# Which of a chunk's four score groups feeds its maximum to the exponential as a bias: from the first to the third

## The chip, the cores and the metric

The kernel runs on one core of a Trainium2 chip. The metric is the time of one execution on the device in microseconds.

## What is computed

The reference takes x of shape (16, 1024, 256): 16 sequences of 1024 tokens with 256 features. Each of two layers computes `x = x + s * g`, with s an attention and g a SiLU of a feed-forward network, both on the normalised x. The first layer has gated linear attention and eight experts; the second has the attention that the change touches, and a feed-forward network with a squared ReLU. The second attention, cut to what matters:

```python
# 16 query heads of 16, 2 key heads, a window of 64 keys around each query
q = (x @ Wq + bq).reshape(b, s, 16, 16).transpose(0, 2, 1, 3)
k, v = ...                       # 2 heads, padded by 32 on both sides
k_win, v_win = kp[:, :, idx], vp[:, :, idx]      # idx = s + (0..63)
scores = einsum('bgrsd,bgswd->bgrsw', qg, k_win)
probs = softmax(scores, axis=-1)
out = einsum('bgrsw,bgswd->bgrsd', probs, v_win)
return out.reshape(...) @ Wo + bo
```

A softmax row needs its maximum taken off before the exponential; the sum of the exponentials comes out of the product with the values, which carry a column of ones, and is divided out at the end.

## The kernel before

One sequence after the other goes through the whole program. Each engine has its own instruction list, written out by hand in program order (eight sequences are unrolled in the text, and that text runs twice); an engine waits on counted semaphores (`pe.wait_ge(s["pr_ok"], ...)`), each raised by one engine. TensorE's list is the longest; the other engines feed it.

In the second attention a sequence is 8 chunks of 128 tokens. A chunk's scores lie in four PSUM banks, 1 to 4, one for each group j = 0 to 3 of four heads, 96 keys wide for each head. Per chunk:

- TensorE, `score_masks(c)` (L1683): four bf16 matmuls, one for each bank and each on 32 rows of the array, write the window mask; before each it waits until the bank's old scores have been read. Then `score_quad(c)` (L1694): 64 small fp32 matmuls, 16 for each bank, in the order bank 1, 2, 3, 4, bank 1, ...
- VectorE, `shifted(n)` with n = 4c + j: the maximum of each row and head (L1322), and, for three of the four groups, the difference score minus maximum (L1329) into SBUF (`pr`, called am in the profile).
- ScalarE, `exps(n)`: for these three groups one exponential over 128x384 of `pr` in place (L991). For the remaining group, whose maximum was taken negated, four exponentials over 128x96 straight from the bank, with the maximum as the bias (L997), one for each head.
- TensorE, `probs_turn(c, p)` (L1708): transposes groups 0 and 1 (p = 0) or 2 and 3 (p = 1); ScalarE copies the result out in two pieces, `probs_turned` (L1007). TensorE multiplies with the values, `values(c)` (L1727); ScalarE copies that out, `values_out` (L1015); TensorE turns it back, `values_turn` (L1740); VectorE divides by the sums (L1338, L1342).
- TensorE, `attention_turn` (L1747) and `attention_project` (L1753): the output projection, with a ScalarE copy between them, `attention_turned` (L1022).

The seven turns of the loop are in this order. TensorE in turn c: `score_masks(c+1)`, `score_quad(c+1)`, `attention_turn(c-1)`, `probs_turn(c,1)`, `attention_project(c-1)`, `values(c)`, `probs_turn(c+1,0)`, `values_turn(c)`, and for c < 3 `window_values(c+1)` (L1665: eight transposes for the values of later chunks). ScalarE in turn c: `attention_turned(c-1)`, two `probs_turned`, `exps(4c+4)`, `exps(4c+5)`, `values_out(c)`, `exps(4c+6)`, `probs_turned`, `exps(4c+7)`, `probs_turned`. After the loop the feed-forward network begins with `hidden(0, 0)` (L1793, L1798) into the same banks, its ReLU on ScalarE (L1074), the square on GpSimd, a split on ScalarE and VectorE (L1053, L1397), and `project` (L1810).

Of the kernel before, what the change touches and what calls it, by code (L numbers as in the profile page):

```python
# [16 lines left out]
ALU = mybir.AluOpType  # L17
ACT = mybir.ActivationFunctionType
AX = mybir.AxisListType
# [5 lines left out]
NC = S // P  # L25
# [23 lines left out]
def build_program(nc, a, out, n_seq):  # L49
# [3 lines left out]
    def sb(name, shape, dt=F32):  # L53
        return ctx.enter_context(nc.sbuf_tensor(name, shape, dt))

    def sem(name):
        return ctx.enter_context(nc.semaphore(name))
# [129 lines left out]
    row_max = sb("row_max", [P, 4, 4])  # L187
# [101 lines left out]
    s = {n: sem(n) for n in names}  # L289
# [36 lines left out]
    def at(name, value=0):  # L326

        return now["copy"] * per_sequence[name] + value
# [379 lines left out]
    with nc.Fori(0, n_seq // UNROLL) as turn:  # L708
        with nc.Block() as block:
# [124 lines left out]
            def _(act):  # L834
                for copy in range(UNROLL):
# [150 lines left out]
                    def exps(n):  # L986

                        c, j = n // 4, n % 4
                        if j:
                            act.wait_ge(s["sub_ok"], at("sub_ok", 3 * c + j))  # L990
                            nc.scalar.activation(pr[:, j], pr[:, j], ACT.Exp).then_inc(s["pr_ok"], 1)  # L991
                            return
                        act.wait_ge(s["max_ok"], at("max_ok", n + 1))
                        if c:
                            act.wait_ge(s["ptp_ok"], at("ptp_ok", 4 * c - 2))
                        for h in range(4):
                            ins = nc.scalar.activation(pr[:, j, h, :], bank[1 + j][:, h * KW:(h + 1) * KW], ACT.Exp,  # L997
                                                       bias=row_max[:, j, h:h + 1])
                        ins.then_inc(s["pr_ok"], 1)
# [18 lines left out]
                    def attention_turned(c):  # L1018
                        act.wait_ge(s["o2tp_ok"], at("o2tp_ok", c + 1))
                        if c:  # L1020
                            act.wait_ge(s["s2p_ok"], at("s2p_ok", c))
                        nc.scalar.copy(o2t[:], bank[0][:, 0:D])\  # L1022
                          .then_inc(s["o2t_ok"], 1)

                    exps(0)
                    queries_keys(3)
                    exps(1)
                    queries_keys(4)
                    exps(2)
                    queries_keys(5)  # L1030
                    exps(3)
# [83 lines left out]
            def _(dve):  # L1115
                for copy in range(UNROLL):
# [198 lines left out]
                    def shifted(n):  # L1315

                        c, j = n // 4, n % 4
                        scored = bank[1 + j][:, 0:4 * KW].rearrange("p (h k) -> p h k", k=KW)
                        dve.wait_ge(s["sc_ok"], at("sc_ok", n + 1))
                        if j == 0 and c:  # L1320
                            dve.wait_ge(s["pr_ok"], at("pr_ok", 4 * c - 3))
                        nc.vector.tensor_reduce(row_max[:, j, :], scored, AX.X, ALU.max, negate=(j == 0))\  # L1322
                          .then_inc(s["max_ok"], 1)
                        if j == 0:
                            return
                        dve.wait_ge(s["max_ok"], at("max_ok", n + 1))
                        if c:
                            dve.wait_ge(s["ptp_ok"], at("ptp_ok", 4 * (c - 1) + 2 * (j // 2) + 2))
                        nc.vector.tensor_tensor(pr[:, j], scored, row_max[:, j, :].unsqueeze(2).broadcast_to([P, 4, KW]),  # L1329
                                                ALU.subtract).then_inc(s["sub_ok"], 1)  # L1330
# [15 lines left out]
                    def attention_bias(c):  # L1346
                        dve.wait_ge(s["s2p_ok"], at("s2p_ok", c + 1))
                        nc.vector.tensor_tensor(attn2[:, c, :], bank[0][:, D:2 * D], bc_o2[:], ALU.add)\
                          .then_inc(s["s2_ok"], 1)

                    shifted(0)
                    window_values(0)
                    for n in range(1, 4):
                        shifted(n)
                    for c in range(NC - 1):
                        shifted(4 * c + 4)
                        shifted(4 * c + 5)
                        shifted(4 * c + 6)
                        if c:
                            attention_bias(c - 1)  # L1360
                        shifted(4 * c + 7)
                        attention_out(c)
                        if c < 3:
                            window_values(c + 1)
                        if c in (1, 2):

                            g = c - 1
                            nc.vector.tensor_copy(xh[:, g], xt[:, :, g * 512:(g + 1) * 512]).then_inc(s["xh_ok"], 1)  # L1368
                        if 3 <= c < 7:
                            low_split((c - 3) // 2, (c - 3) % 2)  # L1370
# [55 lines left out]
            def _(pe):  # L1426
                for copy in range(UNROLL):
# [247 lines left out]
                    def score_masks(c):  # L1675

                        for j in range(4):
                            if c and j == 0:
                                pe.wait_ge(s["pr_ok"], at("pr_ok", 4 * c - 3))
                            elif c:  # L1680
                                pe.wait_ge(s["sub_ok"], at("sub_ok", 3 * c - 3 + j))
                            rows = slice(j * WB, (j + 1) * WB)
                            nc.tensor.matmul(bank[1 + j][:, 0:4 * KW], four_bf[rows, :],  # L1683
                                             band_q[rows, :].unsqueeze(1).broadcast_to([WB, 4, KW]),
                                             start=True, stop=False, skip_group_check=True)
# [81 lines left out]
                    chunk_turn(NC - 1)  # L1767
                    pe.wait_ge(s["qk2_ok"], at("qk2_ok", 4))
                    score_masks(0)
                    score_quad(0)  # L1770
                    window_values(0)
# [5 lines left out]
                    def hidden(n, part):  # L1777

                        g, m = n // MT, n % MT
                        h_bank = bank[1 + n % 3][:]  # L1780
                        if part == 0:
                            if n >= 3:
                                pe.wait_ge(s["relu_ok"], at("relu_ok", n - 2))
                            else:
                                if n == 0:
                                    pe.wait_ge(s["pr_ok"], at("pr_ok", 4 * NC - 3))
                                else:
                                    pe.wait_ge(s["sub_ok"], at("sub_ok", 3 * NC - 3 + n))
                            if m == 0:
                                pe.wait_ge(s["xl_ok"], at("xl_ok", g + 1))  # L1790
                            for t in (xh, xl):
                                for k in range(KD):
                                    nc.tensor.matmul(h_bank, fc_t[:, k, m * P:(m + 1) * P], t[:, g, k, :],  # L1793
                                                     start=(t is xh and k == 0), stop=False)
                        else:
                            if m == 0:
                                pe.wait_ge(s["tst_ok"], at("tst_ok", g + 1))
                            nc.tensor.matmul(h_bank, u_t[:, m * P:(m + 1) * P], t_st[:, g, :], start=False, stop=True)\  # L1798
                              .then_inc(s["h2p_ok"], 1)
# [29 lines left out]
                    for c in range(NC - 1):  # L1829
                        score_masks(c + 1)  # L1830
                        score_quad(c + 1)
                        if c:
                            attention_turn(c - 1)
                        probs_turn(c, 1)
                        if c:
                            attention_project(c - 1)
                        else:
                            low_rank(1)
                        values(c)
                        probs_turn(c + 1, 0)  # L1840
                        values_turn(c)
                        if c < 3:
                            window_values(c + 1)
                    hidden(0, 0)
                    hidden(0, 1)
                    attention_turn(NC - 2)
                    probs_turn(NC - 1, 1)
                    hidden(1, 0)
                    hidden(1, 1)
                    attention_project(NC - 2)  # L1850
# [62 lines left out]
```

## Time and profile before

| | |
|---|---|
| time, three runs | 3715.4, 3718.62 and 3726.18 us, median 3718.62 |
| the profiled execution | 3713.08 us, of it 3711.4 us span |
| TensorE matmuls busy | 92% of the span |
| VectorE, ScalarE, GpSimd busy | 68%, 52%, 34% |
| granted TensorE clock | 0.994 on average |

Busy time is the time in which an engine runs instructions; the span is from the first instruction to the last. The granted clock is a share of full speed.

### The profile page before, as it was taken

Reading aid. Unit: us, or ns where it says so; the run is one execution under the profiler, and the core shown is the slowest. Engines: PE = TensorE matmul, PEld = TensorE weight load, DVE = VectorE, ACT = ScalarE, POOL = GpSimd, SP = SyncE. Lnnn points to the kernel's source line nnn. Section 1 sums busy time; section 2 is a strip of 40 time slices with the busy share of each in tenths; the row PEclk is TensorE's granted clock in tenths of the full one; section 3 lists DMA queues with packets and bytes.
Section 4 is the critical chain, followed back from the end, with each engine's and each line's share of the span. In section 5 each row is a group of like instructions: output and inputs, shape, how many; then the busy total and the mean of one; then the engine's idle time right before and its main releaser. Section 6 shows DMA issues by size and latency. Waiting matters only on the chain. (4 is left out here: it accounts for less than half of the span.)

```text
span 3711.4 us, 89270 instructions
## 1 busy us (share of the span) xinstructions
PE 3420.2 (92%) x34684; PEld 2299.6 (62%) x34684; DVE 2515.5 (68%) x6040; ACT 1928.1 (52%) x4295; POOL 1279.9 (34%) x1489
## 2 busy tenths in 40 slices
PE   3999999999999999999989999999999999999998
PEld 2666666666666666666656666666666666666666
DVE  4666776667677666677656776677666767676667
ACT  2365462645636465463644636546364563646546
POOL 3523324232342423325223251332424234242332
PEclk9999999999999999999999999999999999999999
DMA  3101010010100101001010010101001010010100
GB/s 86 24 14 46 2 39 20 14 46 2 47 13 18 42 14 35 13 24 35 14 36 13 24 35 14 47 2 38 21 15 45 2 47 13 18 42 14 35 13 24
DMA packets 91022, 97.16 MB, mean 26 GB/s; under 512 B 19824, under 2 KB 73696, under 8 KB 90592
## 3 DMA queue, kind: packets, MB, share of 16 engines
q1 hardware_dynamic: 90592, 91.35, 9.1%
q8 instruction: 279, 4.57, 0.5%
q14 instruction: 151, 1.24, 0.1%
HBM read 74.01 MB, written 17.30 MB: 25 GB/s over the span
## 5 line engine op out<-in xcount | busy, mean ns | idle before, releaser
L827 POOL TENSOR_TENSOR qx<-qx 128x512 f32<-128x512 f32 x256 | 278.1, 1091 | 680.3 <-ACT qx L1074 679.4
L1322 DVE TENSOR_REDUCE row_max<-bank 128x4 f32<-128x384 f32 x512 | 271.9, 549 | 134.7 <-PE bank L1694 134.2
L1202 DVE TENSOR_TENSOR am<-bank,causal 128x512 f32<-128x512 f32 x512 | 327.2, 680 | 43.2 <-PE bank L1543 43.2
L1397 DVE TENSOR_TENSOR sq_lo<-qx,sq_hi 128x512 fp32r<-128x512 f32 x256 | 208.0, 813 | 198.4 <-ACT sq_hi L1053 197.9
L925 ACT ACTIVATE tanh_g<-bank 128x256 f32<-128x256 f32 x128 | 49.1, 383 | 468.4 <-PE bank L1432 468.4
L1432 PE MATMUL bank<-w_vg,xt 128*128 128x512 f32 x512 | 253.9, 618 | 0.0
L821 POOL TENSOR_TENSOR xl<-xt,xh 128x1024 fp32r<-128x1024 f32 x32 | 75.3, 2354 | 469.2 <-DVE xh L1368 469.2
L1473 PE MATMUL bank<-xt,w_down 128*128 128x512 f32 x512 | 235.5, 592 | 0.0
L1810 PE MATMUL bank<-sq_hi,pj_t 128*128 128x512 f32 x512 | 214.7, 419 | 16.4 <-DVE sq_lo L1397 9.9
L1329 DVE TENSOR_TENSOR am<-bank,row_max 128x384 f32<-128x384 f32 x384 | 214.0, 557 | 13.1
L744 POOL TENSOR_TENSOR qx<-qt,par_mask 128x512 f32<-128x512 f32 x128 | 139.2, 1088 | 194.9 <-ACT qt L447 155.4
L991 ACT ACTIVATE am<-am 128x384 f32<-128x384 f32 x384 | 206.4, 538 | 0.0
L1074 ACT ACTIVATE qx<-bank,scale_fc 128x512 f32<-128x512 f32 x256 | 177.3, 693 | 50.7 <-PE bank L1798 50.7
L1708 PE MATMUL bank<-ident,am 64*96 64x64 f32 x4096 | 166.9, 221 | 38.8 <-ACT am L991 24.1
L1810 PE MATMUL bank<-sq_lo,pj_t 128*128 128x512 f32 x512 | 202.2, 395 | 0.0
L1708 PEld LDWEIGHTS bank<-ident,am 64*96 64x96 f32 x4096 | 130.5, 123 | 104.1 <-issue 54.3
L1053 ACT CAST sq_hi<-qx 128x512 fp32r<-128x512 f32 x256 | 158.9, 621 | 67.4 <-PE bank L1810 36.8
L940 ACT ACTIVATE tanh_f<-bank 128x256 f32<-128x256 f32 x128 | 49.3, 385 | 239.6 <-PE bank L1574 239.6
L1543 PE MATMUL bank<-qx,k 32*128 32x256 f32 x2048 | 146.6, 400 | 28.2 <-ACT k L844 17.8
L1793 PE MATMUL bank<-xh,fc_t 128*128 128x512 f32 x512 | 171.2, 415 | 0.0
L1694 PE MATMUL bank<-k,qt 32*32 32x192 f32 x8192 | 164.1, 332 | 0.0
L1793 PE MATMUL bank<-xl,fc_t 128*128 128x512 f32 x512 | 160.3, 394 | 0.0
(258 smaller groups left out, 8709.1 us busy)
## 6 DMA issues: line engine op xcount, KB each, us to landing
g_wide<-gate_rows SPq DMA_DIRECT2D x64, 512.0 KB, 6.5
qt<-in_L_attn_x SPq DMA_DIRECT2D x136, 128.0 KB, 2.3
x<-in_L_attn_x SPq DMA_DIRECT2D x128, 128.0 KB, 2.2
out<-x SPq DMA_DIRECT2D x128, 128.0 KB, 1.7
x<-in_L_ffn_w_fc SPq DMA_DIRECT2D x1, 1024.0 KB, 5.6
attn<-in_L_ffn_w_proj SPq DMA_DIRECT2D x1, 1024.0 KB, 7.9
w_up<-in_L_ffn_Wu SPq DMA_DIRECT2D x1, 512.0 KB, 5.8
w_down<-in_L_ffn_Wd SPq DMA_DIRECT2D x2, 256.0 KB, 3.5
```

The source lines that it names most:

```text
L827: nc.gpsimd.tensor_tensor(sq[:, n % 3, :], relu[:, n % 3, :], relu[:, n % 3, :], ALU.mult)\
L991: nc.scalar.activation(pr[:, j], pr[:, j], ACT.Exp).then_inc(s["pr_ok"], 1)
L1074: nc.scalar.activation(relu[:, n % 3, :], bank[1 + n % 3][:], ACT.Relu, scale=scale_fc[:, n % MT:n % MT + 1]).then_inc(s["relu_ok"], 1)
L1202: nc.vector.tensor_tensor(am_tiles[:, :, j], bank[3 + j][:].rearrange("p (f e t) -> p f e t", f=2, e=2), causal[:].unsqueeze(1).unsqueeze( ...
L1322: nc.vector.tensor_reduce(row_max[:, j, :], scored, AX.X, ALU.max, negate=(j == 0))\
L1329: nc.vector.tensor_tensor(pr[:, j], scored, row_max[:, j, :].unsqueeze(2).broadcast_to([P, 4, KW]), ALU.subtract).then_inc(s["sub_ok"], 1)
L1397: nc.vector.tensor_tensor(sq_lo[:, n % 3, :], sq[:, n % 3, :], sq_hi[:, n % 3, :].bitcast(F32), ALU.subtract)\
L1432: mm = nc.tensor.matmul(dst, xt[:, k, c * P:(c + 1) * P], w[:, k, :], start=(k == 0), stop=(k == KD - 1))
L1473: mm = nc.tensor.matmul(bank[5 if g else j][:], w_down[:, k, j * P:(j + 1) * P], xt[:, k, g * 512:(g + 1) * 512], start=(k == 0), stop=(k ...
L1708: mm = nc.tensor.transpose(bank[5 + r][0:KW, h * QB:(h + 1) * QB], pr[rows, 2 * p + h // 4, h % 4, :], ident[rows, rows])
L1793: nc.tensor.matmul(h_bank, fc_t[:, k, m * P:(m + 1) * P], t[:, g, k, :], start=(t is xh and k == 0), stop=False)
L1810: mm = nc.tensor.matmul(bank[5 + o][:], pj_t[:, m, o * P:(o + 1) * P], part[:, n % 3, :], start=(m == 0 and part is sq_hi), stop=(m == MT ...
```

## The change

The group that takes its maximum as a bias, and so needs no difference on VectorE, is j = 2 where it was j = 0. For group 0 VectorE now computes the difference, and its exponential is one instruction; for group 2 the difference goes, and its exponential is four instructions from PSUM bank 3. The waits follow: a mask for bank 3 (and, after the last chunk, the first matmul of `hidden(2, 0)`) waits for ScalarE's exponential, the one for bank 1 for VectorE's difference. The order in which the groups come on each engine stays.

```diff
@@ exps(n) on ScalarE
                         c, j = n // 4, n % 4
-                        if j:
-                            act.wait_ge(s["sub_ok"], at("sub_ok", 3 * c + j))
+                        if j != 2:
+                            act.wait_ge(s["sub_ok"], at("sub_ok", 3 * c + min(j + 1, 3)))
                             nc.scalar.activation(pr[:, j], pr[:, j], ACT.Exp).then_inc(s["pr_ok"], 1)
                             return
                         act.wait_ge(s["max_ok"], at("max_ok", n + 1))
                         if c:
-                            act.wait_ge(s["ptp_ok"], at("ptp_ok", 4 * c - 2))
+                            act.wait_ge(s["ptp_ok"], at("ptp_ok", 4 * c))
                         for h in range(4):
                             ins = nc.scalar.activation(pr[:, j, h, :], bank[1 + j][:, h * KW:(h + 1) * KW], ACT.Exp,
                                                        bias=row_max[:, j, h:h + 1])
@@ shifted(n) on VectorE
                         dve.wait_ge(s["sc_ok"], at("sc_ok", n + 1))
-                        if j == 0 and c:
-                            dve.wait_ge(s["pr_ok"], at("pr_ok", 4 * c - 3))
-                        nc.vector.tensor_reduce(row_max[:, j, :], scored, AX.X, ALU.max, negate=(j == 0))\
+                        if j == 2 and c:
+                            dve.wait_ge(s["pr_ok"], at("pr_ok", 4 * c - 1))
+                        nc.vector.tensor_reduce(row_max[:, j, :], scored, AX.X, ALU.max, negate=(j == 2))\
                           .then_inc(s["max_ok"], 1)
-                        if j == 0:
+                        if j == 2:
                             return
@@ score_masks(c) on TensorE
                         for j in range(4):
-                            if c and j == 0:
-                                pe.wait_ge(s["pr_ok"], at("pr_ok", 4 * c - 3))
+                            if c and j == 2:
+                                pe.wait_ge(s["pr_ok"], at("pr_ok", 4 * c - 1))
                             elif c:
-                                pe.wait_ge(s["sub_ok"], at("sub_ok", 3 * c - 3 + j))
+                                pe.wait_ge(s["sub_ok"], at("sub_ok", 3 * c - 3 + min(j + 1, 3)))
@@ hidden(n, 0) on TensorE
-                                if n == 0:
-                                    pe.wait_ge(s["pr_ok"], at("pr_ok", 4 * NC - 3))
+                                if n == 2:
+                                    pe.wait_ge(s["pr_ok"], at("pr_ok", 4 * NC - 1))
                                 else:
-                                    pe.wait_ge(s["sub_ok"], at("sub_ok", 3 * NC - 3 + n))
+                                    pe.wait_ge(s["sub_ok"], at("sub_ok", 3 * NC - 2 + n))
```

On ScalarE, one whole turn of the loop, from the copy of `attention_turned` to the last `probs_turned`. Before:

```order
L1022 COPY o2t<-bank 128x256
L1007 COPY xn<-bank 96x8x64 x2
L997 ACTIVATE am<-bank,row_max 128x96 x4
L991 ACTIVATE am<-am 128x384
L1015 COPY o_turned<-bank 128x4x4x32
L991 ACTIVATE am<-am 128x384
L1007 COPY qx<-bank 96x8x64
L991 ACTIVATE am<-am 128x384
L1007 COPY qx<-bank 96x8x64
```

With the change, the same turn:

```order
L1022 COPY o2t<-bank 128x256
L1007 COPY xn<-bank 96x8x64 x2
L991 ACTIVATE am<-am 128x384 x2
L1015 COPY o_turned<-bank 128x4x4x32
L997 ACTIVATE am<-bank,row_max 128x96 x4
L1007 COPY qx<-bank 96x8x64
L991 ACTIVATE am<-am 128x384
L1007 COPY qx<-bank 96x8x64
```

The four small exponentials have moved from ahead of `values_out` (o_turned) to behind it; what stood behind them up to `values_out` now follows one exponential, and what follows the third group's exponential now follows four.

On VectorE, the four groups of one chunk, from the first maximum up to the division for the chunk before (the row L1348 is the bias of the output projection). Before:

```order
L1322 TENSOR_REDUCE row_max<-bank 128x4 x2
L1329 TENSOR_TENSOR am<-bank,row_max 128x384
L1322 TENSOR_REDUCE row_max<-bank 128x4
L1329 TENSOR_TENSOR am<-bank,row_max 128x384
L1348 TENSOR_TENSOR attn<-bank,bc_o 128x256
L1322 TENSOR_REDUCE row_max<-bank 128x4
L1329 TENSOR_TENSOR am<-bank,row_max 128x384
L1338 RECIPROCAL rden<-bank 128x16
```

With the change:

```order
L1322 TENSOR_REDUCE row_max<-bank 128x4
L1329 TENSOR_TENSOR am<-bank,row_max 128x384
L1322 TENSOR_REDUCE row_max<-bank 128x4
L1329 TENSOR_TENSOR am<-bank,row_max 128x384
L1322 TENSOR_REDUCE row_max<-bank 128x4
L1348 TENSOR_TENSOR attn<-bank,bc_o 128x256
L1322 TENSOR_REDUCE row_max<-bank 128x4
L1329 TENSOR_TENSOR am<-bank,row_max 128x384
L1338 RECIPROCAL rden<-bank 128x16
```

The difference of the first group now stands ahead of the second group's maximum, and the third group's difference is gone; five instructions still stand ahead of L1348. TensorE's instructions and their order are the same.

## Rows read from the trace of the kernel before

**Rows 1.** Page, part 1: busy time of the engines, share of the span, instructions
```profile
PE 3420.2 (92%) x34684; PEld 2299.6 (62%) x34684; DVE 2515.5 (68%) x6040; ACT 1928.1 (52%) x4295; POOL 1279.9 (34%) x1489
```

**Rows 2.** Page, part 4: the chain that ended last, by line
```profile
PE bank L1473 3%; PE bank L1571 3%; PE bank L1432 2%; PE bank L1793 2%; PE bank L1708 2%; PE bank L1654 2%; PE bank L1694 2%; PE bank L1614 2%; PE bank L1453 2%; ACT am L997 2%; DMA g_wide<-gate_rows 1%; PE bank L1810 1%; PE bank L1543 1%; PE bank L1528 1%; PE bank L1740 1%
```

**Rows 3.** Waits: engine, line, whom it waited for; total us, times, longest
```profile
PE bank L1708 <- ACT am L991: 24.1, 96, 0.3
```

**Rows 4.** Timeline, turn c = 5 and the next: start us, length us, engine, line
```profile
246.78 1.02 DVE L1322 TENSOR_REDUCE row_max<-bank 128x4 f32<-128x384 f32 x2
247.83 0.56 DVE L1329 TENSOR_TENSOR am<-bank,row_max 128x384 f32<-128x384 f32 x1
...
248.70 1.03 ACT L997 ACTIVATE am<-bank,row_max 128x96 f32<-128x96 f32 x4
...
248.86 1.08 PE L1727 MATMUL bank<-xn,v 96*32 96x128 f32 x32
...
249.60 0.54 ACT L991 ACTIVATE am<-am 128x384 f32<-128x384 f32 x1
...
250.02 0.59 ACT L1015 COPY o_turned<-bank 128x512 f32<-128x512 f32 x1
...
250.19 0.65 PE L1708 MATMUL bank<-ident,am 64*96 64x64 f32 x16 [0.25 <-ACT am L991]
250.28 0.56 DVE L1329 TENSOR_TENSOR am<-bank,row_max 128x384 f32<-128x384 f32 x1
250.49 0.54 ACT L991 ACTIVATE am<-am 128x384 f32<-128x384 f32 x1
...
250.77 0.66 PE L1740 MATMUL bank<-ident,o_turned 128*128 128x128 f32 x4
...
251.36 0.34 PE L1683 MATMUL bank<-band_q,four_bf 32*128 32x384 bf16 x4
...
251.63 1.28 PE L1694 MATMUL bank<-k,qt 32*32 32x192 f32 x64
...
253.22 0.65 PE L1708 MATMUL bank<-ident,am 64*96 64x64 f32 x16
```

**Rows 5.** Timeline, turn c = 0 of the same sequence
```profile
216.44 1.08 PE L1727 MATMUL bank<-qx,v 96*32 96x128 f32 x32
...
217.45 0.65 PE L1708 MATMUL bank<-ident,am 64*96 64x64 f32 x16
217.59 0.58 ACT L1015 COPY o_turned<-bank 128x512 f32<-128x512 f32 x1
...
218.23 0.65 PE L1740 MATMUL bank<-ident,o_turned 128*128 128x128 f32 x4
```

**Rows 6.** Timeline, turn c = 1, where window_values follows values_turn
```profile
223.05 1.08 PE L1727 MATMUL bank<-xn,v 96*32 96x128 f32 x32
...
224.97 0.66 PE L1740 MATMUL bank<-ident,o_turned 128*128 128x128 f32 x4
...
226.13 0.34 PE L1683 MATMUL bank<-band_q,four_bf 32*128 32x384 bf16 x4
```

**Rows 7.** Timeline, turn c = 6, the last, and what follows it
```profile
255.02 1.08 PE L1727 MATMUL bank<-qx,v 96*32 96x128 f32 x32
...
257.97 0.60 ACT L1007 COPY xn<-bank 96x512 f32<-96x512 f32 x1
...
258.90 0.65 PE L1708 MATMUL bank<-ident,am 64*96 64x64 f32 x16
```

**Rows 8.** Timeline, the one named wait of TensorE in the feed-forward network, 259 to 282 us
```profile
278.02 0.50 PE L1810 MATMUL bank<-sq_hi,pj_t 128*128 128x512 f32 x1 [0.24 <-DVE sq_lo L1397]
```

**Rows 9.** Timeline, the sequence's first chunk: its third exponential, and the next masks
```profile
209.86 0.51 ACT L991 ACTIVATE am<-am 128x384 f32<-128x384 f32 x1
...
211.47 0.34 PE L1683 MATMUL bank<-band_q,four_bf 32*128 32x384 bf16 x4
```

## The prediction

> **What bounds the kernel now.** The page's busy shares come first: TensorE is busy for 92% of the span, the next engine for 68% [rows 1]. So a change is worth what it does to the start times of TensorE's instructions, and nothing else. The chain that ended last runs mostly through TensorE's lines, and one line that the change moves stands in it: L997, the four small exponentials, with 2% of 3711 us, some 74 us [rows 2]. It is one of the few places where ScalarE, not TensorE, sets the pace. The waits then say how much of that is idle time: TensorE waits before the transposes of `probs_turn` (L1708) for the exponential L991 in 96 places, 24.1 us in all, 0.25 us each [rows 3]. 96 is 16 sequences by six of the loop's seven turns. The timeline of one turn says why, and what comes after it; all that follows is read from there.
>
> Take T as the start of `values(c)` on TensorE, 248.86 in turn 5 [rows 4]. ScalarE begins the four small exponentials at 248.70 and ends them at 249.73; the second group's exponential ends at 250.14, and `probs_turn(c+1,0)` starts 0.05 us later, at 250.19. The values' matmuls had ended at 249.94. That is the 0.25 us. But behind `probs_turn` TensorE needs `values_out`, which ScalarE can't begin before the values are done: 250.02 to 250.61. `values_turn` starts at 250.77, only 0.16 us after it. The masks start at 251.36 (T + 2.50), the scores at 251.63, and 6.16 us after T the next values start, at 255.02 [rows 7].
>
> **The change, part by part.**
>
> Work: VectorE still has four maxima and three differences a chunk, ScalarE four small and three large exponentials, TensorE the same list. Nothing is added or removed; only times move.
>
> (a) The first two exponentials. They cost 0.54 us each where the first cost 1.03, with 0.42 us from one start to the next (249.60 to 250.02) [rows 4]. If ScalarE begins at 248.70 as before, the second ends at 248.70 + 0.42 + 0.54 = 249.66, before the values' end at 249.94, so the 0.25 us wait is gone. Condition: VectorE must have both differences ready. The first maximum starts at 246.78; two maxima take 1.02 us, a difference 0.56 [rows 4]. Maximum, difference, maximum, difference at 0.56 us each at most end by 249.02. ScalarE wants the second difference at 249.12. The cover is 0.1 us, and behind it the 0.28 us by which the exponential is now early (249.66 against 249.94); it holds.
>
> (b) What TensorE gets of the 0.25 us. `values_turn` can't start before `values_out` is copied, and turn 0 shows what happens without the wait: `probs_turn` starts with the values' end, at 217.45, ScalarE copies from 217.59, and `values_turn` starts at 218.23, 1.79 us after the values [rows 5]. With the wait it is 1.91 (248.86 to 250.77) or 1.92 (223.05 to 224.97) [rows 4, 6]. So the gain is 0.13 us a turn, half of the wait.
>
> (c) What the third group's exponential now holds. It starts 0.47 us after `values_out`'s start, at T + 1.63 (250.49). Before, no one on TensorE waited for it: the last difference on VectorE, 250.28 to 250.84, had freed the last bank, half a microsecond before the masks. Now it is four instructions, 1.03 us, to T + 2.66, and the mask for bank 3 may start at T + 2.71. Before, the masks started at T + 2.50 [rows 4]. Behind this mask in TensorE's list stand the fourth mask, the 64 score matmuls, and all of the next turn. So where nothing stands between `values_turn` and the masks, they come 0.21 us late, with the gain of (b) already eaten. These are the masks behind turns 3, 4 and 5: three in a sequence. The first two masks go ahead at T + 2.37. That could help only if the scores could then follow in less than the 0.27 us that they now stand behind the masks (251.36 to 251.63). The profile gives the four masks as one group of 0.34 us, so I read them as running side by side, each for most of the 0.34, and the 0.27 us as running time, not issue time. I take the whole 0.27 again behind the late mask. The lower bound: a quarter of it for each of two masks, 0.13, so 0.07 us late instead of 0.21. The upper bound: the two late masks don't run together any more but one behind the other, another 0.27: 0.48 us late.
>
> The Trainium skill, TensorEngine Tiling (Array Packing), Key Properties, says that changing the tiling mode drains the engine, and also that tiles within a mode load and run independently. Masks are 32x128 and scores 32x32, so by the first rule no score starts before the late mask is through: 0.21 us. By the second alone the scores of banks 1 and 2 would run ahead, and the cost would be near the lower bound. The trace agrees with the first as far as it goes, with its 0.27 us between masks and scores [rows 4].
>
> (d) Turns 1 and 2. There `window_values` stands between `values_turn` and the masks, which start at T + 3.08 (223.05 to 226.13) [rows 6]. Moved up by 0.13 they start at T + 2.95, still after T + 2.71. So these turns keep the gain: twice -0.13. If that cover were gone it would cost +0.21 there as well.
>
> (e) Turn 0 has no wait to lose, and keeps its time [rows 5]. The first chunk: its third exponential, 209.86 to 210.37, would last to 210.89, and the masks start at 211.47 [rows 9]; nothing.
>
> (f) Turn 6. Behind it come the first hidden matmuls, which need bank 1, free early. But `probs_turn(7,1)` needs the fourth `probs_turned` copy, to clear its banks. Before, that copy starts at T + 2.95 and ends at T + 3.55 (257.97, 0.60), and the transposes start at T + 3.88 (258.90) [rows 7]. Now the copy stands behind four small exponentials, that is 0.90 - 0.42 = 0.48 us later (248.70 to 249.60 is the step behind four small ones, 249.60 to 250.02 that behind a large one [rows 4]): it ends at T + 4.02, the transposes start at T + 4.07. So +0.19. In turns 3 to 5 the same copy is also late, but there `probs_turn(c+1,1)` stands at T + 4.36 (253.22) [rows 4], which has cover of 0.3 us, and more once the masks are late. The feed-forward network behind it shows TensorE with one named wait up to 282 us, 0.24 us [rows 8]; it is fed by a chain that starts from TensorE too, so I let the delay run through.
>
> Sum for a sequence: -0.13 x 2 + 0.21 x 3 + 0.19 = +0.56 us; by 16, +9.0 us. Against the profiled execution: 3713.1 + 9.0 = 3722.1. That execution lies 5.5 us under the median of the runs shown, 3718.6; against the median it is 3727.6, and I say 3727. It is +0.24%; about 0.3%, 11.2 us, is what a measurement of this kernel can tell from no change.
>
> **Rivals.**
>
> Forecast (54%): the gains of two turns, the losses of three and of the end. Its own range: with 0.17 to 0.27 for the held masks, +7 to +12 us, so about one case in four of it lies above 0.3%.
>
> Held masks are cheap (15%): 0.07 us instead of 0.21. Sum -0.26 + 0.21 + 0.19 = +0.14, by 16 +2 us: 3721. For it speaks that two of the four masks and their rows of the array are free early; against it, that the scores of the late rows need as long as the others' and are issued in order.
>
> Faster (8%): the third exponential holds no one, because it starts earlier than I have it. Then six turns give 0.13 us each, by 16 -12.5 us: 3706; were the whole wait to come off, -24.1 [rows 3], 3694. It decides if that exponential ends 0.2 us earlier than T + 2.66. Against it: `values_out` stands ahead of it and waits for the values' end.
>
> Slower, the masks torn apart (15%): the wait in the middle of the four masks costs more than its length, 0.48 us a time by the upper bound. That is 0.27 x 3 x 16 = +13 us on top, +22 in all: 3740. For it speaks that the four now start as one group; against it, that the third and fourth are still released together. It passes 0.3% from 0.26 us for a held mask (the sum is then -0.26 + 0.78 + 0.19 = +0.71, by 16 +11.4).
>
> Slower, the first wait stays (8%): the second difference on VectorE comes over 0.4 us later than I have it, since the first is now ahead of it, and `probs_turn` waits on. The gain of turns 1 and 2 is gone: (0.63 + 0.19) x 16 = +13 us: 3732.
>
> **How the numbers follow.** Slower by over 0.3%: 0.15 + 0.08 + a quarter of 0.54, 0.36. Faster: 0.08. Within: 0.56. The range from 3711 to 3739 leaves out the faster rival and the last microsecond or so of the torn masks, and holds the cheap masks (3721), the forecast and the wait that stays (3732). It goes 10 us below the cheap masks and 7 above the stayed wait, since the three runs before lie 11 us apart.
>
> **What the profile after would show.** The 96 waits of L1708 for L991 gone; in turns 1 to 6 `values_turn` 1.79 us behind the values. A new wait at the masks L1683 for L997, 48 times, some 0.2 to 0.35 us each (the first masks at T + 2.37, the rest at T + 2.71), and a distance between values of turns 3 to 6 of 6.37 us where it was 6.16, and 0.13 us less in turns 1 and 2. L1708 after turn 6 waiting for a copy of L1007, 16 times, 0.2 to 0.3 us. I am wrong if the masks start within 0.05 us of T + 2.50 in turns 3 to 5, if their wait is there and the scores still follow at T + 2.84 or earlier, or if the feed-forward network gives the delay back before the sequence ends.

## The result: slower, by more than the moved waits

The changed kernel takes 3755.18 us (median of four, 3751.93 to 3757.93), the kernel before 3719.7 (median of four): a ratio of 1.0094, with a 95% interval from 1.0076 to 1.0111. The prediction was 3727, from 3711 to 3739. It had the direction; the measured loss, 35 us, is about four times the forecast one. The profiled execution takes 3757.93 us, 3756.2 of it span, 44.8 us more span than before.

The profile after, first by the same views. The page, part 1, and from part 5 the matmuls of L1571 in the first layer; then the same group before, which was not shown above (busy us, mean ns of one, idle before it):

```profile
PE 3470.1 (92%) x34684; PEld 2330.9 (62%) x34684; DVE 2515.7 (67%) x6040; ACT 1940.4 (52%) x4295; POOL 1279.9 (34%) x1489
...
L1571 PE MATMUL bank<-w_up,qx 128*128 128x256 f32 x512 | 134.5, 410 | 33.5 <-POOL qx L786 33.5
```

```profile
L1571 PE MATMUL bank<-w_up,qx 128*128 128x256 f32 x512 | 125.4, 389 | 32.7 <-POOL qx L786 32.7
```

TensorE has the same 34684 matmuls, but is busy for 50 us more [rows 1]. Idle time is not what grew. And matmuls in another layer, which the change doesn't touch, have become longer, while they wait for GpSimd hardly longer than they did. That is the first sign that something beside the waits has moved.

The waits (engine, line, whom for; total us, times, longest):

```profile
PE bank L1708 <- ACT qx L1007: 14.7, 16, 0.9
PEld bank L1683 <- ACT am L997: 12.2, 48, 0.3
...
PE bank L1708 <- ACT xn L1007: 5.4, 16, 0.3
```

The 96 waits of [rows 3] are gone. The 48 waits before the masks are there, 0.25 us each, and the 16 behind turn 6, 0.34 us each. The first of the three rows is the old wait in turn 0, with the same 14.7 us as before.

The timeline of TensorE in turns 1 to 4 and 6 answers to [rows 4, 6, 7]:

```profile
223.46 1.08 PE L1727 MATMUL bank<-xn,v 96*32 96x128 f32 x32
...
230.07 1.08 PE L1727 MATMUL bank<-qx,v 96*32 96x128 f32 x32
...
236.68 1.08 PE L1727 MATMUL bank<-xn,v 96*32 96x128 f32 x32
...
238.47 0.66 PE L1740 MATMUL bank<-ident,o_turned 128*128 128x128 f32 x4
239.05 0.68 PE L1683 MATMUL bank<-band_q,four_bf 32*128 32x384 bf16 x4
239.67 1.28 PE L1694 MATMUL bank<-k,qt 32*32 32x192 f32 x64
...
243.05 1.08 PE L1727 MATMUL bank<-qx,v 96*32 96x128 f32 x32
...
255.79 1.08 PE L1727 MATMUL bank<-qx,v 96*32 96x128 f32 x32
...
259.96 0.65 PE L1708 MATMUL bank<-ident,am 64*96 64x64 f32 x16 [0.34 <-ACT xn L1007]
```

From T = 236.68 of turn 3: `values_turn` at T + 1.79, the masks from T + 2.37 and now 0.68 us long as a group, since two of them wait in the middle and start at T + 2.72 (the row of their weight load below); the scores at T + 2.99, 0.22 later than T + 2.77 before; the next values at T + 6.37, where it was 6.16. Turn 1 lasts 6.61 us (6.74 before, from 223.05 to 229.79). Behind turn 6 the transposes stand at T + 4.17.

```profile
239.40 0.09 PEld L1683 LDWEIGHTS bank<-band_q,four_bf 32*128 32x128 bf16 x2 [0.26 <-ACT am L997]
```

So the moved waits do almost what the prediction says. They explain a quarter of the loss. The rest shows when the granted clock is read stretch by stretch. Windows of TensorE after the change, from the first sequence's first masks (L1683) on, for about two sequences (stretch, its length, busy us and instructions, then PEclk, the granted clock as a share of full speed, and the DMA engines' share and GB/s). I call a stretch at 0.50 a low stretch:

```profile
203.80:339.90 136.10, 128.16 (x1476) 1.00 0.12 33
339.90:343.30 3.40, 3.40 (x15) 0.50 0.02 5
343.30:415.00 71.70, 68.71 (x597) 1.00 0.07 16
415.00:418.40 3.40, 3.40 (x39) 0.50 0.02 5
418.50:568.60 150.10, 139.81 (x1517) 1.00 0.11 30
568.70:572.00 3.30, 3.30 (x13) 0.50 0.00 0
572.00:643.70 71.70, 68.70 (x597) 1.00 0.07 16
643.70:647.10 3.40, 3.40 (x39) 0.50 0.00 0
```

The clock falls from 2.4 to 1.2 GHz (1.00 to 0.50) twice between one sequence's first masks and the next one's, 136 and 211 us after them. Both times TensorE is by then in the first layer of the sequence that comes next. What TensorE does just before each, in the timeline after:

```profile
336.23 0.38 PE L1592 MATMUL bank<-ident,k 128*128 128x128 f32 x2
338.66 2.58 PE L1571 MATMUL bank<-w_up,qx 128*128 128x256 f32 x8 [2.04 <-POOL qx L786]
...
414.58 0.84 PE L1608 MATMUL bank<-qt,state_mid 128*128 128x128 f32 x4 [2.28 <-DVE am L1202]
```

and the same two places before:

```profile
337.55 1.99 PE L1571 MATMUL bank<-w_up,qx 128*128 128x256 f32 x8 [1.99 <-POOL qx L786]
...
411.89 0.71 PE L1608 MATMUL bank<-qt,state_mid 128*128 128x128 f32 x4 [2.28 <-DVE am L1202]
```

TensorE waits 2 us, for GpSimd at the first place and for VectorE at the second, and starts again; here the clock falls 1.2 and 0.4 us later. The waits are not new, and they are hardly longer. These are their rows after (total us, times, longest), with the next longest wait of the layer, at L1560, and then the same rows before:

```profile
PE bank L1608 <- DVE am L1202: 37.3, 18, 2.3
...
PE bank L1560 <- DVE xn L1195: 21.4, 16, 1.3
```

```profile
PE bank L1608 <- DVE am L1202: 37.2, 18, 2.3
...
PE bank L1560 <- DVE xn L1195: 21.3, 16, 1.3
```

Each of the 16 sequences has one long wait at L1608, 2.26 to 2.29 us in both kernels, and one at L1571, 1.92 to 2.29 us before and 1.97 to 2.32 after.

Leave out the first layer of the very first and of the ninth sequence, where the text of eight starts anew and the clock falls in both kernels. In the 14 stretches from first masks to first masks that remain, the clock before stayed up behind the first wait throughout and fell behind the second in five. After, it falls behind both waits in 13 of the 14 and behind neither in one: 26 times. No low stretch in these 14 begins behind the wait of 1.3 us. Sequence by sequence, in windows from first masks to first masks, after:

```profile
2729.50:2958.30 228.80, 215.56 (x2163) 0.99 0.09 25
2958.40:3183.70 225.30, 212.28 (x2162) 1.00 0.09 25
3183.80:3412.40 228.60, 215.55 (x2164) 0.99 0.09 25
```

and before:

```profile
203.50:428.20 224.70, 211.24 (x2163) 1.00 0.09 25
428.30:654.70 226.40, 212.73 (x2163) 0.99 0.09 25
654.80:879.40 224.60, 211.20 (x2163) 1.00 0.09 25
```

By the first masks' starts a sequence with the clock up lasts 224.75 us before (nine of them, 224.73 to 225.01) and 225.41 after (the only one): that is what the moved waits cost, 0.66 us. With one low stretch it is 226.4 before, with two 228.68 after: (228.68 - 225.41) / 2 = 1.63 us for each. The sum: 16 x 0.66 = 10.6, and 26 - 5 = 21 low stretches more at 1.63 are 34.2; together 44.8, the difference of the spans. That it meets to the tenth is luck, since each term is good to 1 or 2 us.

### The profile page after: what moved, and what is told of

Read it like the earlier page. It is cut to its first block and busy times, and to the rows that moved or that the text cites. A ratio compares the mean times of both kernels' runs of the same rounds, so it can differ in the third digit from the quotient of the medians.

```text
span 3756.2 us, 89270 instructions
## 1 busy us (share of the span) xinstructions
PE 3470.1 (92%) x34684; PEld 2330.9 (62%) x34684; DVE 2515.7 (67%) x6040; ACT 1940.4 (52%) x4295; POOL 1279.9 (34%) x1489
## 5 line engine op out<-in xcount | busy, mean ns | idle before, releaser
L991 ACT ACTIVATE am<-am 128x384 f32<-128x384 f32 x384 | 191.9, 530 | 30.2 <-DVE am L1329 30.2
L1708 PE MATMUL bank<-ident,am 64*96 64x64 f32 x4096 | 166.9, 221 | 20.1 <-ACT qx L1007 14.7
L1571 PE MATMUL bank<-w_up,qx 128*128 128x256 f32 x512 | 134.5, 410 | 33.5 <-POOL qx L786 33.5
```

What stands on the lines that cost most here:

```text
L1571: nc.tensor.matmul(bank[up_banks[c]][:, 0:D], hidden_t[c // 4][:, j, c % 4 * P:(c % 4 + 1) * P], w_up[:, j, :], start=(j == 0), stop=False)
L1708: mm = nc.tensor.transpose(bank[5 + r][0:KW, h * QB:(h + 1) * QB], pr[rows, 2 * p + h // 4, h % 4, :], ident[rows, rows])
```

## The experiments

Two theories. **A**: the waits of the change cost some 11 us; the rest is the clock, which falls behind two old waits of the first layer, and how often it does so is decided by how long a sequence lasts. **B**: the clock falls because of the change's own waits, those in the middle of the masks above all.

The experiments ran on three chips; each ratio is against the kernel before on the same chip, which takes 3717.18 us (before_masks2, after_masks2, after_masks4, mixed), 3718.56 (before_masks3 and the kernels with 8 filling matmuls) and 3717.23 (before_masks4 and those with 4). The counts are of low stretches behind the two waits in the same 14 stretches, each in one profiled execution.

| kernel | sequence, clock up | low stretches | median us | ratio |
|---|---|---|---|---|
| before | 224.75 | 5 | 3717 to 3720 | 1 |
| after | 225.41 | 26 | 3755.2 | 1.0094 |
| before_masks2 | 225.2 | 2 | 3720.2 | 1.0010 |
| before_masks3 | 225.3 | 10 | 3740.9 | 1.0070 |
| before_masks4 | 225.6 | 26 | 3752.9 | 1.0088 |
| after_masks2 | 225.9 | 20 | 3749.6 | 1.0085 |
| after_masks4 | none seen | 20 | 3761.8 | 1.0125 |
| mixed | 224.7 | 6 | 3714.3 | 0.9993 |
| before_fill | 226.9 | 0 | 3735.5 | 1.0046 |
| after_fill | 227.6 | 0 | 3745.7 | 1.0076 |
| mixed_fill | 226.7 | 0 | 3731.2 | 1.0037 |
| before_fill4 | 224.9 | 0 | 3702.5 | 0.9958 |
| after_fill4 | 225.6 | 0 | 3713.3 | 0.9988 |
| mixed_fill4 | 224.6 | 0 | 3698.8 | 0.9947 |

### Sequences made longer, without and with the change's waits

Every mask matmul starts its bank anew, so writing the same masks again only takes time. In `score_masks(c)`, behind the four masks; the counts by chunk are {2: 1, 3: 1} for two, {2: 1, 3: 2} for three and {2: 2, 3: 2} for four more groups:

```diff
+                        for _ in range({2: 1, 3: 1}.get(c, 0)):
+                            for j in range(4):
+                                rows = slice(j * WB, (j + 1) * WB)
+                                nc.tensor.matmul(bank[1 + j][:, 0:4 * KW], four_bf[rows, :], ...,
+                                                 start=True, stop=False, skip_group_check=True)
```

> The kernel before, with the four masks of chunks 2 and 3 written twice: 0.27 us more each, +0.54 us a sequence, close to the +0.66 us that the change costs a sequence where the clock stays up, and without any of its waits. Theory A (the rest of the loss is the clock, which falls behind two long waits of TensorE in the first layer when a sequence has this length): low stretches about 136 and 211 us after a sequence's first masks in nearly every sequence, time near 3755 us. Theory B (the clock falls because TensorE pauses between the masks, or because of the other waits of the change): as few low stretches as before, time near 3720 + 9 = 3729 us.

Measured: 3720.22 us, 1.0010 (1.0000 to 1.0019), and 2 low stretches. A's number, 3755, is wrong, B's, 3729, is nearer. The +3 us are less than the 0.47 us a sequence that the masks add, 7.5 us; three low stretches fewer, some 5 us, make up nearly all of the rest. An undisturbed sequence is 225.2 us long, not the 225.4 of the changed kernel. So the run didn't make the case that it was meant to make. The next two close the gap.

> The kernel before with three more groups of four masks a sequence: about +0.75 us a sequence (two more gave 0.47), +12 us of work, none of the change's waits. A sequence without a low stretch then lasts about 225.5 us, the 225.4 of the changed kernel. Theory A (how long a sequence lasts decides whether the clock falls at the two long waits): low stretches 136 and 211 us after a sequence's first masks in most sequences, time 3745 to 3765 us. Theory B (the change's own waits make it fall): at most the 5 of before behind the first sequence, time 3717 + 12 = 3729 us.

Measured: 3740.86 us, 1.0070 (1.0050 to 1.0089), executions from 3731 to 3750. The profiled one has 10 low stretches, in five sequences with both. The median is under A's range and well over B's number. A sequence lasts 225.3 us with the clock up; here the clock falls in some sequences and not in others.

> The kernel before with four more groups of masks a sequence. Two more made an undisturbed sequence 225.2 us long, three more 225.3 (before: 224.75), so four make it about 225.6. Theory A (the length of a sequence decides): as in the changed kernel with its 225.4, low stretches at +136 and +211 us in most sequences, 3750 to 3762 us. Theory B: 3717 + 14 = 3731 us.

Measured: 3752.91 us, 1.0088 (1.0073 to 1.0104), as A has it. Its sequences look like those of the changed kernel, in windows from first masks to first masks (the last of them is one with the clock up):

```profile
203.50:432.20 228.70, 215.16 (x2179) 0.99 0.09 25
432.30:660.90 228.60, 215.02 (x2179) 0.99 0.09 25
661.00:889.70 228.70, 215.11 (x2179) 0.99 0.09 25
2043.00:2268.50 225.50, 211.93 (x2179) 1.00 0.09 25
```

It has none of the change's waits: there is no wait before the masks beyond the old issue gaps, and the old wait of the transposes is in its place (here L1714):

```profile
PE bank L1714 <- ACT am L991: 24.5, 96, 0.3
```

So 0.8 us of plain work in a sequence brings the clock down 26 times, as the change does. B is wrong: the change's own waits aren't needed for it.

> The changed kernel with the masks of chunks 2 and 3 written twice: +0.54 us a sequence, +9 us of work. Theory A: the sequence no longer has the length at which the clock falls twice each time, so fewer low stretches, and the time is below 3755 in spite of more work, 3730 to 3750 us. Theory B: the pauses between the masks are still there, so as many low stretches, and 3755 + 9 = 3764 us.

Measured: 3749.64 us, 1.0085 (1.0068 to 1.0102), 20 low stretches. The kernel does more work than the changed one and takes no longer, inside A's range, at its upper end. B's 3764 is excluded; so is 3761, which B's number becomes on this chip (3717.18 x 1.0094 + 9), since the interval ends at 3755.

> The changed kernel with the masks of chunks 2 and 3 written three times: +1.08 us a sequence, +17 us of work. Theory A: few low stretches; 3720 + 11 + 17 = 3748 us plus at most 20 us for the low stretches that are left. Theory B: 3755 + 17 = 3772 us.

Measured: 3761.83 us, 1.0125 (1.0109 to 1.0142), 20 low stretches. Inside A's range, 10 us below B's number. But on this chip B's number becomes 3769, and the interval ends at 3770, so this time alone doesn't decide between the two; the 20 low stretches, where B has 26, are all that speaks against B here.

### The two waits filled

If the clock falls behind the two waits because TensorE has nothing to do in them, matmuls put there should keep it up. Bank 2 and the first half of bank 7 are free at these places, and are written anew right after (excerpts from two places):

```diff
                         if part == 0:
+                            if c == 0:
+                                for _ in range(8):
+                                    nc.tensor.matmul(bank[2][:, 0:D], w_up[:, 0, 0:P], w_up[:, 0, :],
+                                                     start=True, stop=True, skip_group_check=True)
                             pe.wait_ge(s["hm_ok"], at("hm_ok", c + 1))
...
+                        if c == NC - 1:
+                            for _ in range(8):
+                                nc.tensor.matmul(bank[7][:, 0:D], w_up[:, 0, 0:P], w_up[:, 0, :],
+                                                 start=True, stop=True, skip_group_check=True)
                         pe.wait_ge(s["am_ok"], at("am_ok", 4 * c + 4))
```

> The changed kernel with 8 matmuls, whose result is overwritten, put into each of the two long waits of TensorE in the first layer (2.04 us for GpSimd ahead of L1571, 2.28 us for VectorE ahead of L1608), where the low stretches begin. Theory A: the low stretches at +136 and +211 us are gone, and the time is that of before plus the direct cost, 3717 + 11 = 3728 us, less some 8 us for the low stretches that before has too: 3720 to 3730 us. Theory B: the low stretches stay, 3755 us or, with the filling in the way, more.

> The kernel before with the same filling. Theory A: its 5 low stretches behind the first sequence go, 1.6 us each: 3717 - 8 = 3709 us, if the filling itself fits into the waits. Theory B: no change, 3717 us.

> The version with the third group as bias in chunks 2 and 3 alone, with the same filling. Theory A and the steps of the prediction: 4 us below before_fill, 3705 us. Theory B: as mixed, 3714 us.

Measured: 3745.68, 3735.52 and 3731.19 us. All three are above what was expected, for a reason that the timeline of after_fill shows:

```profile
335.54 3.62 PE L1569 MATMUL bank<-w_up 128*128 128x256 f32 x16
339.00 1.89 PE L1575 MATMUL bank<-w_up,qx 128*128 128x256 f32 x8
```

Each fp32 matmul stands as two in the profile, so 8 take 3.6 us where the wait was 2. But the low stretches at both places are gone in all three, and so the differences between the three are free of the clock. After minus before: 3745.68 - 3735.52 = 10.2 us. Mixed (below) minus before: -4.3 us. The prediction's terms are +9.0 and -0.26 x 16 = -4.2.

With 4 matmuls instead of 8 the filling fits:

> The changed kernel with 4 matmuls in each of the two long waits instead of 8. The 8 took 3.5 us a wait, more than the wait; 4 take 1.7 and fit. Theory A: no low stretches behind the first sequence's, and no cost: 3709 + 11 = 3720 us. Theory B, or if the 0.3 to 0.5 us of wait that is left is enough for the clock to fall: 3755 us.

> The kernel before with 4 matmuls in each of the two waits. Theory A: 3717 - 8 = 3709 us, for 5 low stretches less of 1.6 us each. Theory B: 3717 us.

Measured: after_fill4 3713.33 us, 0.9988 (0.9979 to 0.9998); before_fill4 3702.53 us, 0.9958 (0.9943 to 0.9974). No low stretch is left at either place, sequences of after_fill4 in the same windows:

```profile
200.50:426.40 225.90, 215.89 (x2179) 1.00 0.09 25
426.40:651.90 225.50, 215.87 (x2179) 1.00 0.09 25
651.90:877.30 225.40, 215.85 (x2179) 1.00 0.09 25
```

The changed kernel with 8 matmuls of waste in each sequence is some 40 us faster than without (1.0094 and 0.9988 of the kernel before), and a little faster than the kernel before. Its distance to before_fill4 is 10.8 us, where it was 10.2 with 8 matmuls a wait. Both are 6 to 7 us below their expectation: in the very first and in the ninth sequence a low stretch has gone as well, which the count of 5 left out. before_fill4 reaches its first masks at 200.6 us (203.5 before), and that one long sequence lasts 236.0 us, not 238.7. These 5.6 us are more than two low stretches cost; what the rest comes from was not looked into.

### The third group only where window_values covers it

The group with the bias is chosen by chunk: j = 2 in chunks 2 and 3, and j = 0 in all others. The masks that overwrite the scores of chunks 2 and 3 are those of chunks 3 and 4, and they come behind `window_values`. The main lines of the edit:

```diff
+BG = [2 if c in (2, 3) else 0 for c in range(NC)]
...
+def subs(c, j):
+    return 3 * c + (j if BG[c] == 0 else min(j + 1, 3))
...
-                        if j:
-                            act.wait_ge(s["sub_ok"], at("sub_ok", 3 * c + j))
+                        if j != BG[c]:
+                            act.wait_ge(s["sub_ok"], at("sub_ok", subs(c, j)))
...
-                            if c and j == 0:
-                                pe.wait_ge(s["pr_ok"], at("pr_ok", 4 * c - 3))
+                            if c and j == BG[c - 1]:
+                                pe.wait_ge(s["pr_ok"], at("pr_ok", 4 * c - 3 + j))
```

> The third group takes the bias in chunks 2 and 3 alone, where window_values covers the masks' wait; the first in all other chunks. By my steps -0.13 us in turns 1 and 2, and no held masks and no late copy at the end: -0.26 us a sequence, -4 us, 3716 us, if the clock falls as rarely as before (5 low stretches behind the first sequence's). If the gain of the two turns does not exist: 3720 us.

Measured: 3714.26 us, 0.9993 (0.9983 to 1.0003). The 3 us are of the expected sign and size, but the interval holds 1. The turns themselves show the gain; from T to T it is 6.61 us in turns 1 and 2, where turn 1 lasted 6.74 before:

```profile
222.88 1.08 PE L1732 MATMUL bank<-xn,v 96*32 96x128 f32 x32
...
229.49 1.08 PE L1732 MATMUL bank<-qx,v 96*32 96x128 f32 x32
...
236.10 1.08 PE L1732 MATMUL bank<-xn,v 96*32 96x128 f32 x32
```

> The third group as bias in chunks 2 and 3 alone, with 4 matmuls in each of the two waits. 4 us below before_fill4, as mixed_fill was below before_fill: 3705 us, and so faster than the kernel before (3717) by 0.3%.

Measured: 3698.83 us, 0.9947 (0.9934 to 0.9961), the fastest of all. It is 3.7 us below before_fill4, as forecast, and 6 us below its number, for the same reason as the other two. No execution of it, or of mixed_fill, lies in the range of its partner. Its rows at the first filled wait, and at the second:

```profile
332.08 1.89 PE L1574 MATMUL bank<-w_up 128*128 128x256 f32 x8
334.32 1.99 PE L1580 MATMUL bank<-w_up,qx 128*128 128x256 f32 x8 [0.35 <-POOL qx L791]
...
408.64 0.71 PE L1621 MATMUL bank<-qt,state_mid 128*128 128x128 f32 x4 [0.55 <-DVE am L1207]
```

The filling ends before GpSimd and VectorE are ready, so it costs nothing, and the clock stays up behind the 0.35 and 0.55 us of wait that are left.

## Why the prediction was wrong

**(a), the first wait.** Right. The 96 waits are gone.

**(b), 0.13 us a turn of them.** Right: `values_turn` is at T + 1.79, by turn 0's pattern [rows 5].

**(c), the held masks.** Right in place, number and size: 48 waits; the prediction's T + 2.37 for the first masks, 6.37 us from values to values. The scores stand at T + 2.99, where T + 2.98 follows from the whole 0.27 us behind the late mask. The lower bound, scores at T + 2.84, is excluded, and so is the rival of the torn masks. One reading behind it was wrong: the 0.27 us are not all running time of the masks. Where before_masks2 writes the masks twice, the second four start 0.17 us behind the first, and only the scores stand 0.26 us behind:

```profile
219.32 0.34 PE L1683 MATMUL bank<-band_q,four_bf 32*128 32x384 bf16 x4
219.49 0.33 PE L1689 MATMUL bank<-band_q,four_bf 32*128 32x384 bf16 x4
219.75 1.28 PE L1700 MATMUL bank<-k,qt 32*32 32x192 f32 x64
```

So about 0.1 us is added where the tile shape changes. The Trainium skill (TensorEngine Tiling (Array Packing), Key Properties) states that changing the tiling mode drains the engine, and that different tiles can work in parallel. The trace agrees with the drain as far as this 0.1 us goes, and no score ran ahead of the late masks. That would also follow if TensorE starts matmuls in the order of its list; no run separates the two.

**(d), (e), turns 1, 2 and 0.** Right: 6.61 us for turns 1 and 2, and turn 0 keeps its 6.61.

**(f), the late copy behind turn 6.** Right in place, mis-sized: T + 4.17 instead of 4.07, so +0.29 for +0.19. The copy ends when forecast, at 259.81 (259.22 and 0.59, from the same timeline), and TensorE starts 0.15 us behind it, not 0.05. These 0.10 us a sequence, 1.6 us in all, are the whole difference between the sum of the steps and what they cost.

**The sum of the steps.** +0.56 us a sequence was forecast and +0.66 measured, 9.0 and 10.6 us. Two pairs of kernels in which the clock stays up at the two places give 10.2 and 10.8 us. None of the rivals (cheap masks, faster, torn masks, a stayed wait) happened.

**What failed** is a term that the sum puts at nothing, by the first paragraph's conclusion: "So a change is worth what it does to the start times of TensorE's instructions, and nothing else." Every duration in the sum was taken over from before, at a granted clock of 0.994, and no rival had a term for the clock. The clock was the largest term: 21 low stretches of 1.63 us, 34 of the 45 us, in which the matmuls themselves take longer (389 to 410 ns for those of L1571). Low stretches were in the trace before, too, in about one sequence of three, behind a wait of TensorE of 2.3 us. Nothing in the rows chosen for the prediction shows them.

What the runs show of this term: filling the two waits removes it (all six filled kernels, the changed one with its mask waits among them), and lengthening the sequence without any new wait brings it (before_masks4). What they leave open is why the same two waits bring the clock down in a sequence of 225.4 or 225.6 us nearly each time (26 of 28), in one of 225.9 less often (20), in one of 225.3 now and then (10), in one of 225.2 hardly ever (2), and in one of 224.75 at the second place alone, five times. A longer sequence alone is no rule: the count goes up and down with the length. The distances are alike from sequence to sequence; in the changed kernel the first low stretch of a sequence starts 228.7 us behind that of the one before (339.9, then 568.6), which is also the length of a sequence with two low stretches. So each sequence may meet the same state as the one before. That the clock's fall depends on when in time the wait comes is my reading of this; no run here varies the time alone.

## What to carry to other kernels

Read the granted clock in windows, not only as a mean, and look at what TensorE does ahead of each low stretch: a kernel with regular waits of 2 us in a busy stream lost 1% here through a change of less than 1 us a sequence elsewhere. A difference of that size between two variants is no evidence on the edit until the low stretches of both are counted. Where such a wait can't be removed, a few matmuls of waste that fit into it settled the matter here, and they also make variants comparable: with them the +10.6 us of the change's steps came out as 10.2 and 10.8, and the -4.2 us of mixed as -4.3 and -3.7.

## What was unexpected of the hardware

Waits of 2.04 and 2.28 us, in a stream that is busy for 94% of the time (128.16 of 136.10 us), were followed by a fall from 2.4 to 1.2 GHz, for 3.4 us and at a cost of 1.63 us. The same waits in the kernel before mostly were not. The Trainium skill (TensorE: Matmul & The Clock Gate, HAM oscillation) describes a clock that goes down again and again in a loop of short bursts and waits for a transfer, in a kernel that is far from busy. Here it happens in a kernel that is at 92%, twice in 228 us. What is left of the two waits in the fill4 kernels, 0.35 and 0.55 us in the rows of mixed_fill4, was never followed by a low stretch.
